# A four-stage conv/attention block on one core: the value product is issued between the scores and the weights

## The reference

```
L0: q,k,v = qkv(x); q,k = rope(q,k); out = softmax(q k^T / 4) v; proj     (12 heads of 16, 1024 tokens)
L1: in_proj, 3x3 conv, silu, four-direction selective scan, layernorm, gate, out_proj
L2: like L0 without rope, scores + rel_h[q, k_row] + rel_w[q, k_col]
L3: like L0, but each token sees its 7x7 neighbourhood only
```

## Time and profile before

| | us |
|---|---|
| median of 3 runs | 9652.29 (9651.52 to 9661.92) |
| the profiled execution | 9689.28 |
| its span, first to last instruction | 9687.5 |
| PE busy | 7431.7 (77%) |
| DVE busy | 5231.6 (54%) |
| ACT busy | 3265.7 (34%) |

### The profile page before, as it was taken

The page is one execution under the profiler, slowest core; times in us unless marked ns, Lnnn a source line. Parts: engine busy times, 40 slices in busy tenths (PEclk is TensorE's granted clock), DMA queues, the critical chain, the costliest instruction groups (busy, mean ns, idle before and its releaser), DMA issues.

```text
span 9687.5 us, 102786 instructions
## 1 busy us (share of the span) xinstructions
PE 7431.7 (77%) x32648; PEld 2984.0 (31%) x32648; DVE 5231.6 (54%) x5444; ACT 3265.7 (34%) x3578; POOL 1465.9 (15%) x700
## 2 busy tenths in 40 slices
PE   6779777797777977779777797777977779777797
PEld 1233322333223332233322333223332233322332
DVE  6565355653556536564365643656436564365643
ACT  3323333243332433324333243332433324333243
POOL 0230002300023010220102200022000220002200
PEclk9778887788877988778887788877888778887788
DMA  2001110011100111001110011100111001110011
GB/s 60 7 25 33 42 44 7 26 32 43 44 6 26 32 45 43 5 27 32 45 42 5 26 32 45 42 5 27 32 45 42 5 26 32 45 42 5 27 32 48
DMA packets 158935, 298.44 MB, mean 31 GB/s; under 512 B 48974, under 2 KB 56390, under 8 KB 158378
## 3 DMA queue, kind: packets, MB, share of 16 engines
q1 hardware_dynamic: 158378, 291.44, 10.1%
HBM read 185.75 MB, written 83.50 MB: 28 GB/s over the span
## 4 chain that ended last, share of the span: by engine, by line
PE 53%; DVE 19%; issue 8%; DMA 7%; DVEq 5%; ACT 4%; SPq 3%; POOL 1%; ACTq 0%; POOLq 0%
PE px L606 10%; PE ring L556 6%; PE ring L583 6%; PE px L1026 4%; DVE mx L763 4%; PE ring L559 4%; PE ring L1010 4%; DMA ks<-k_split 4%; DVE hs L1243 3%; PE ring L585 3%; PE ring L982 3%; PE ring L997 2%; PE ring L535 2%; PE ring L475 2%; DVEq L778 2%
## 5 line engine op out<-in xcount | busy, mean ns | idle before, releaser
L763 DVE TENSOR_REDUCE mx<-ring 128x1 f32<-128x1024 f32 (+1 forms) x1920 | 2158.7, 1141 | 2044.6 <-PE ring L559 971.5
L676 ACT ACTIVATE pt<-ring 128x1024 f32<-128x1024 f32 (+1 forms) x1920 | 1872.2, 981 | 2612.5 <-PE ring L585 1114.2
L823 POOL TENSOR_TENSOR os<-oe 64x512 f32<-64x512 f32 x288 | 364.9, 1267 | 6544.0 <-ACT oe L684 6544.0
L606 PE MATMUL px<-pt,vo 128*32 128x512 f32 (+3 forms) x8064 | 1269.7, 622 | 73.7 <-ACT pt L676 72.3
L556 PE MATMUL ring<-kb,qb 96*128 96x512 bf16 x3072 | 1184.9, 430 | 160.2 <-DVE mx L763 92.6
L1288 POOL TENSOR_TENSOR hc<-hs,crep 128x1024 f32<-128x1024 f32 x384 | 1045.4, 2722 | 1636.5 <-DVE hs L1243 1635.6
L583 PE MATMUL ring<-qb,kb 99*128 99x512 bf16 x3072 | 1121.2, 409 | 179.6 <-DVE mx L763 108.8
L559 PE MATMUL ring<-hot,rq 128*128 128x512 f32 x1536 | 910.3, 654 | 0.0
L1243 DVE TENSOR_TENSOR_SCAN hs<-ring,hs 128x1024 f32<-128x1024 f32 x384 | 874.8, 2278 | 23.7 <-ACT ring L1140 23.7
L585 PE MATMUL ring<-rq,hot 128*128 128x512 f32 x1536 | 861.9, 623 | 0.0
L1010 PE MATMUL ring<-duh,spread 96*128 96x512 f32 x1536 | 606.8, 531 | 285.9 <-DVE hs L1232 142.8
(11 more groups left out here) (153 smaller groups left out, 6729.6 us busy)
## 6 DMA issues: line engine op xcount, KB each, us to landing
qs<-q_split SPq DMA_DIRECT2D x192, 128.0 KB
q_parts<-part SPq DMA_DIRECT2D x96, 192.0 KB, 3.5
k_parts<-part SPq DMA_DIRECT2D x96, 192.0 KB, 2.7
qb<-q_parts SPq DMA_DIRECT2D x192, 96.0 KB
kb<-k_parts SPq DMA_DIRECT2D x192, 96.0 KB
ocm<-os SPq DMA_DIRECT2D x576, 32.0 KB
rb<-reciprocals SPq DMA_DIRECT2D x288, 64.0 KB, 2.2
qb<-q_parts SPq DMA_DIRECT2D x192, 64.0 KB
```

The costliest lines, as they stand in the source:

```text
L606: last = nc.tensor.matmul(m.px[32 * g:32 * g + 32, h % 2, lo - f * HF:hi - f * HF], m.vo[:, t, h, :], pt[:, lo - q0:hi - q0], start=t == t ...
L676: nc.scalar.activation(pt, ps, ACT.Exp, scale=1.0 if L == "C" else HD ** -0.5).then_inc(s.pt, 1)
L763: nc.vector.tensor_reduce(out, ps, AX.X, ALU.max).then_inc(s.mx_used, 1)
```

## The change

In the loop at line 611 the call of `weights(g)` moves behind both calls of `values`, and the condition for a pair's V in A and C goes from even g to odd g:

```diff
             g = n - lead
             if g == 0 and L == "D":
                 pe.wait_ge(m.rows_in, ROWS_IN * b + ROWS_IN)
-            weights(g)
             if L == "D" and g >= 1:
                 values(*divmod(g - 1, steps))
-            if L != "D" and g % 2 == 0 and g >= 2:
+            if L != "D" and g % 2 == 1 and g >= 3:
                 values(*divmod(g // 2 - 1, steps // 2))
+            weights(g)
```

## The result

The changed kernel takes 9711.1 us in the median of 20 runs (9640.9 to 9781.5), the kernel before 9657.7 (9642.5 to 9676.6): a ratio of 1.0055, with a 95% interval of 1.0035 to 1.0075. I had forecast 9462, within 9380 to 9610. It is slower, by half a per cent, and its runs scatter over 141 us where those of the old one scatter over 34.

The account below looks back on a forecast made before the run. PE was taken as the busiest engine, 77% of the span, with holes in A and D and at C's R. Per image -18 (A), -20.4 (C), +14.7 (D), times eight: -190 us, so 9652.3 becomes 9462, range 9380 to 9610.

Parts of the forecast that it names:

- Stage A: Attention stage A: V leaves the loop between W and S; heads of 14.0 us, 18 us an image gained.
- the ring slot: In A, S waits for the slot of the odd W two steps back, a 1.79 us exponential chain; pair 3.32 us.
- the doubtful transition, S to V: In A's new loop, not in the trace: taken as W to V's 0.53 us, bounds 0.44 and 0.7.
- The falls of the clock: In A: none counted, as waits are spread; with the falls kept, 12 us an image instead of 18.
- Stage C: Attention stage C: heads of 24.6 us, a 2.0 us clock fall in one of three; 20.4 us an image gained.
- Both holes: In C: 1.73 us before the second R shrinks to some 0.75; 0.65 before the S behind it grows to 1.8.
- Stage D: Attention stage D: V now stands ahead of W and waits for its exponential; 14.7 us an image lost at full clock.
- The chain: In D, W, exponential, V, W become one chain of 2.38 us a step, with S hidden under the exponential.
- the last steps: D's last eight steps: 1.32 us each becomes 2.38, so 8.5 us an image lost.
- a sign of being wrong: Wrong if A's heads stay near 15 us, C's stay at 27, or D's clock is under 0.8.
- my first rival: Every step of D: the chain brings the low clock, 55 us an image, 9785 us; decides from 38; chance 0.08.
- the first four steps with W: Start of D: these steps lose some 2 us an image, 3.5 at the low clock.

Follow-up runs that it names:

- d_s_twice: The changed kernel with each score matmul of D issued twice into the same place: 9525.5 us, ratio 0.9860 to the kernel before.
- d_filled: d_s_twice plus, in D's steps without S, the weights' matmuls issued once more into the next step's slot: 9485.4 us, ratio 0.9816.

## Why the prediction was wrong

**Stage A: right.** Forecast 14.0 us a head and 18 us an image, measured 13.98 and 18.9. The loop was the predicted one, through the exponential and the ring slot; the doubtful transition, S to V, is the 0.53 that I took. The falls of the clock went, as forecast.

**Stage C: right.** Forecast 24.6 us a head and 20.4 us an image, measured 24.3 and 22.0. Both holes came out within 0.2 us (0.63 for 0.75, 1.63 for 1.8). The clock falls in one head of nine, not in one of three; the rule that the prediction cites from the Trainium skill ("TensorE: Matmul & The Clock Gate", section "Why this matters for your kernels"), by which it would not fall at all, was nearer in number here, though the 1.63 us hole left one fall an image (its start some 1 us behind the hole), which went when V covered it. By that rule a hole of 1.63 us would bring no fall; here the measurement decides. Such a fall cost 1.6 us (25.8 against 24.2), where 2.0 were taken.

**Stage D: the step that failed** is "PE is busy for about 1.6 of 2.38 us, no less dense than in A's last steps, so I take the full clock". The chain was right to 0.01 us (2.37), and the waits for loads that it was to fill did go. But it left the clock at its low level, in half of the images for most of the stage and in the last steps of all. Forecast 14.7 us an image; measured 22 to 27 where the clock holds in the heads and up to 64 where it doesn't, 41 in the mean. Over D, from the first V to the last, the granted clock is 0.50 to 0.89 by image and 0.71 in the mean, below the 0.8 that I had named as a sign of being wrong. This is the mechanism of my first rival, which I gave 0.08: it named 55 us for a stage wholly at the low level (64 measured, mostly since a low step takes 3.42 us and not 3.26), and 38 as the point from which the gains of A and C are gone. The measured mean lies just past that point, and the result follows. That the clock is the cause is shown: extra work in the waits took the low level away (d_s_twice, d_filled), and with the clock held from D's third M on the time is 9485 against my 9462.

Why the argument failed: I compared busy time with busy time, and even so 1.6 of 2.38 us is 67%, a little less than A's 69% and not "no less". The last steps of A are 69% busy and keep the clock; those of D are 64% busy and lose it, and D's heads are 88% busy at 0.50 and don't get it back. Busy time in a profile grows when the clock falls, so it can't tell whether the clock will rise, and A's matmuls are not D's. Which property of them counts no run here tells. I also took the old D's falls, 0.84 in the mean of its window, as a matter of its waits for loads alone. They do follow those waits, and in the images that stay high they are gone. What I didn't ask is how the clock comes back. In the old order a fall in the heads lasted 3 to 10 us and the clock came back each time, in all eight images. Outside the load waits PE is then busy with hardly a hole, as in the first of these windows of the old kernel's second image, and the second is high again:

```profile
2345.00:2348.00 3.00, 3.00 (x11) 1.33 (x9) 1.06 (x2) 1.47 (x4) 0.00 (x0) 0.50 0.21 68
2349.00:2361.00 12.00, 8.93 (x53) 3.76 (x47) 5.01 (x8) 5.93 (x8) 2.25 (x2) 1.00 0.17 52
```

In the new order every low step keeps a hole of about 0.5 us, and no fall in the heads was made good before the stage was over. That the hole is what keeps the clock down fits both, and fits the experiments that filled it, but it isn't shown apart from the amount of work.

A smaller part was mis-sized even in the images whose heads are high, and for the same reason: the last steps cost 13.6 to 18 us an image instead of 8.5, since the clock falls in them, and the first four steps with W 3.6 instead of 2 (12.6 to 16.2 from the second M to the third). All of the latter run at 0.50 in all eight images; 3.5 is what the prediction had named for them at the low clock.

**The scatter** was not forecast at all. A step that has two lengths, of which the long one stays long until the stage is over, makes a time that depends on whether, and when, each stage leaves the upper level.

## What to carry to other kernels

Before a consumer is moved ahead of a producer, write down for every stage that shares the line what the consumer waits for: here one line moved for three stages, won 41 us an image in two and lost 41 in the third, where it closed the chain W, exponential, V. Price a lengthened step at both clock levels, and if its holes recur in every step, give the low level a large chance. Look at the level at which the stage begins, and ask whether the step at the low level still has a hole: the old D's had hardly any and its falls passed, the new one's has one in every step and stays low. And where a wait can't be avoided, have in it work that is needed anyway: V in C's `rq` wait gave 88 us, filler in D's chain 226.

## What the runs showed of the hardware

TensorE's clock can stay at either of its two levels (1.2 and 2.4 GHz) under the same repeated sequence of instructions: at 0.50 for 85 us with PE busy for 74.6 of them and holes of about 0.5 us a step, at 1.00 for 70 us with PE busy for 51.6 and holes of about 0.7. The two are not alike. A stage whose heads were low never came back before its end (15 of the 24 profiled), while a high one fell within the heads in 8 of 17. Doubled scores in the first 20 steps were enough for all eight images of one execution to stay high through the 28 plain ones with S and W that remained, up to the last eight. And a kernel can become faster by doing more: 768 redundant matmuls took 186 us off the changed kernel.

In the 12 us ahead of each fall within the heads of the changed kernel no hole of PE is longer than 0.9 us. That is far shorter than the idle gaps to which the Trainium skill ("TensorE: Matmul & The Clock Gate", section "Why this matters for your kernels") puts such falls; the measurement decides.
